# Down projection with its features on the partitions: wd stationary, activation moving, and the maxima over partitions by VectorE's 32x32 turns

## The reference

```python
gate = x @ W_gate.T + SCALE * (x @ A_gate.T) @ B_gate.T      # A, B by the entry's LoRA index, rank 16
up   = x @ W_up.T   + SCALE * (x @ A_up.T)   @ B_up.T        # 1376 wide
act  = silu(gate) * up
y    = act @ W_down.T + SCALE * (act @ A_down.T) @ B_down.T  # back to 512 features
amax = clip(max(abs(y), axis=-1), 1e-5)                      # one maximum per token, over 512 features
out  = (y / amax) @ weight_2bit.T * (amax * weight_scale) + bias
return x + out
```

## Time and profile before

| | us |
|---|---|
| median of 3 runs | 931.65 (930.52 to 932.57) |
| the profiled execution, its own time | 931.64 |
| its span in the profile | 929.6 |
| TensorE matmuls busy | 892.0 (96%), 3954 matmuls |
| TensorE weight loads busy | 720.6 (78%) |
| VectorE busy | 351.4 (38%) |
| ScalarE busy | 254.4 (27%) |
| GpSimd busy | 79.3 (9%) |

### The profile page before, as it was taken

One profiled execution on the slowest core, in us unless ns is written; L12 is line 12 of the kernel. 1 busy time (PEld: TensorE's weight loads), 2 busy tenths in 40 slices (PEclk: granted clock), 3 DMA queues, 4 the chain that ended last, 5 costly groups with the idle time before them and its releaser, 6 DMA issues.

```text
span 929.6 us, 13785 instructions
## 1 busy us (share of the span) xinstructions
PE 892.0 (96%) x3954; PEld 720.6 (78%) x3954; DVE 351.4 (38%) x762; ACT 254.4 (27%) x448; POOL 79.3 (9%) x110
## 2 busy tenths in 40 slices
PE   4799899999999999999999999999999999999994
PEld 3678688888888888888888888888888888888873
DVE  3543346332542226332363224432254223532233
ACT  2432234211431124211242113421142213421111
POOL 0010002200110001200102001020012000200100
PEclk9899999999999999999999999999999999999998
DMA  3443231120221112111121101101121111100011
GB/s 119 115 132 94 87 85 55 49 52 24 52 57 35 28 29 58 48 41 29 31 55 40 43 23 52 49 23 43 26 55 51 40 28 29 37 12 23 23 35 49
DMA packets 45445, 45.38 MB, mean 49 GB/s; under 512 B 13168, under 2 KB 31984, under 8 KB 45392
## 3 DMA queue, kind: packets, MB, share of 16 engines
q1 hardware_dynamic: 43312, 41.98, 16.7%
q10 hardware_dynamic: 2080, 2.88, 1.0%
HBM read 36.44 MB, written 8.39 MB: 48 GB/s over the span
## 4 chain that ended last, share of the span: by engine, by line
PE 91%; DVE 2%; SPq 2%; DMA 2%; ACT 1%; issue 1%; DVEq 0%; ACTq 0%
PE pp_up L1746 25%; PE pp_gate L1746 23%; PE pp_down L1823 23%; PE ps_misc L1850 5%; PE ps_td L1812 4%; PE ps_misc L1746 2%; PE pp_down L1833 2%; PE pp_up L1793 2%; PE pp_gate L1793 2%; PE ps_misc L1841 1%; DMA rows<-w_gu 1%; SPq L337 1%; DMA x_raw<-x_feat 0%; DMA b_raw<-places 0%; SPq L351 0%
## 5 line engine op out<-in xcount | busy, mean ns | idle before, releaser
L1823 PE MATMUL pp_down<-wd,actp_split 128*128 128x512 f32 x960 | 233.4, 392 | 0.0
L1746 PE MATMUL pp_up<-xw,wgu 128*128 128x512 f32 x948 | 229.3, 391 | 0.0
L1746 PE MATMUL pp_gate<-xw,wgu 128*128 128x512 f32 x864 | 213.6, 396 | 4.5 <-ACT actp_full L968 4.4
L1823 PEld LDWEIGHTS pp_down<-wd,actp_split 128*128 128x128 f32 x960 | 180.4, 188 | 45.0
L1746 PEld LDWEIGHTS pp_up<-xw,wgu 128*128 128x128 f32 x948 | 178.4, 188 | 38.4
L1746 PEld LDWEIGHTS pp_gate<-xw,wgu 128*128 128x128 f32 x864 | 161.2, 189 | 39.1 <-issue 5.7
L1412 DVE TENSOR_TENSOR actp_full<-pp_up,actp_full 128x512 f32<-128x512 f32 (+1 forms) x87 | 60.1, 691 | 329.7 <-PE pp_up L1793 313.4
L968 ACT ACTIVATE actp_full<-pp_gate 128x512 f32<-128x512 f32 (+1 forms) x80 | 47.7, 596 | 286.5 <-PE pp_gate L1793 274.9
L984 ACT ACTIVATE actp_split<-actp_full 128x512 fp32r<-128x512 f32 x80 | 50.6, 632 | 172.4 <-DVE actp_full L1412 172.4
L1421 DVE TENSOR_TENSOR actp_split<-actp_full,actp_split 128x512 fp32r<-128x512 f32 x80 | 55.2, 690 | 16.7 <-ACT actp_split L984 16.7
L1850 PE MATMUL ps_misc<-wq,dtp_split 128*128 128x512 f32 x232 | 57.5, 390 | 0.6 <-DVE dtp_split L1444 0.6
(11 more groups left out here) (112 smaller groups left out, 627.1 us busy)
## 6 DMA issues: line engine op xcount, KB each, us to landing
x_raw<-x_feat SPq DMA_DIRECT2D x122, 64.0 KB, 1.8
rows<-w_gu SPq DMA_DIRECT2D x8, 512.0 KB, 3.7
rows<-x_tok SPq DMA_DIRECT2D x64, 64.0 KB, 1.8
more_rows<-x_tok SPq DMA_DIRECT2D x64, 64.0 KB, 1.8
out<-rows SPq DMA_DIRECT2D x60, 64.0 KB, 1.6
out<-more_rows SPq DMA_DIRECT2D x60, 64.0 KB, 1.6
b_raw<-b_rows SPq DMA_DIRECT2D x32, 92.0 KB, 2.8
b_raw<-b_rows SPq DMA_DIRECT2D x32, 80.0 KB, 2.5
```

The lines of the kernel that those rows point to most:

```text
L1746: return nc.tensor.matmul(ps_out[0:m, a:b], w, xw[:, part, k, a:b], start=start, stop=stop)
L1823: last = nc.tensor.matmul(pp_down[:, s, :], actp_split[0:w, ap, f % 2, s * P:(s + 1) * P], wd[0:w, wp, f, :], start=(f == 1 and n == 0), s ...
```

## The change

`wide_down` and `down_first_and_lora` swap their operands: a 128x128 block of wd is stationary and the activation of all 512 tokens moves. A bank of pp_down (index h) then holds 128 output features on the partitions and 512 tokens along the row, the layout in which `ffn` takes its stationary operand. The count of matmuls and of their columns stays. The `transposes`, the identity's load and ScalarE's `normalise_rows` are gone.

The maximum per token now runs across partitions. VectorE takes it over the four banks (`feature_maxima`: a reduction of 2048 elements per partition to 512), turns 32x32 blocks, reduces 512 to 16, then joins the four groups of partitions (`token_maxima`), and turns the reciprocals back over the partitions (`spread_rinv`); four multiplications scale the banks (`normalise_chunk`). Its scratch is more_rows, so the residual rows of groups 2 and 3 are now loaded behind it (`residual_behind_scratch`, which waits for norm_ready; scratch_free tells VectorE that more_rows is stored). In the last tile the scratch is x_raw. `hi_norm` and `lo_norm` split from SBUF, at f = 2, 4, 6, 8; `ffn` stays at f = 3, 5, 7, 9. `store_wide` reads its entry numbers ahead of its wait.

```diff
+        hidden = rows[:, 0:KC, :]
...
+            entries = [wide_entry_at(eng, tile, (s * P + at) // SEQ) for at in rows_from]
             eng.wait_ge(out_ready, WIDE_SUBS * tile + s + 1)
-            for at in rows_from:
-                entry = wide_entry_at(eng, tile, (s * P + at) // SEQ)
+            for at, entry in zip(rows_from, entries):
...
+            def residual_behind_scratch(tile):
+                entries = [wide_entry_at(sp, tile, e) for e in range(2 * P // SEQ, WIDE_ENTRIES)]
+                sp.wait_ge(norm_ready, KC * tile + KC)
+                for n, entry in enumerate(entries):
+                    s, at = 2 + n * SEQ // P, n * SEQ % P
+                    sp.dma_start(res_rows(s)[at:at + SEQ, :], x_tok[bass.ds(entry, 1), :, :]
+                                 .rearrange("a t n -> (a t) n")).then_inc(res_in[s], 16)
...
-            def normalise_rows(tile, s, source):
-                act.wait_ge(rinv_ready, WIDE_SUBS * tile + s + 1)
-                nc.scalar.activation(norm_rows(s), source, ACT.Copy, scale=rinv[:, s:s + 1]).then_inc(norm_ready, 1)
...
-            def hi_transposed(tile, s, ps_block, dt):
-                act.wait_ge(transposed, WIDE_SUBS * tile + s + 1)
-                nc.scalar.activation(dt[:, 0, :, :], ps_block.rearrange("p (k t) -> p k t", k=KC),
-                                     ACT.Copy).then_inc(dt_hi, 1)
...
+            def drain(tile, h):
+                act.wait_ge(blocks_done, KC * tile + h + 1)
+                nc.scalar.activation(hidden[:, h, :], pp_down[:, h, :], ACT.Copy).then_inc(drained, 1)
...
+            def hi_norm(tile, s, dt):
+                last = isinstance(tile, int) and tile == WIDE_TILES - 1
+                act.wait_ge(norm_ready, KC * tile + (s + 1 if last else KC))
+                if s > 0 and not last:
+                    act.wait_ge(ffn_done, WIDE_SUBS * tile + s)
+                nc.scalar.activation(dt[:, 0, :, :], hidden[:, :, s * P:(s + 1) * P], ACT.Copy).then_inc(dt_hi, 1)
...
+            def feature_maxima(tile):
+                over_chunks, turned = scratch_columns(tile, 0), scratch_columns(tile, 1)
+                if not (isinstance(tile, int) and tile == WIDE_TILES - 1):
+                    dve.wait_ge(scratch_free, tile + 1)
+                dve.wait_ge(drained, KC * tile + KC)
+                maxima_step(tile, 1, nc.vector.tensor_reduce(over_chunks, hidden.rearrange("p h t -> p t h"), AX_X,
+                                                             ALU.max, apply_absolute_value=True))
+                maxima_step(tile, 2, nc.vector.transpose(turned, over_chunks))
+                maxima_step(tile, 3, nc.vector.tensor_reduce(group_max, turned.rearrange("p (c i) -> p c i", i=SEQ),
+                                                             AX_X, ALU.max))
...
+            def token_maxima(tile):
+                for g in range(KC):
+                    last = nc.vector.tensor_copy(by_group[:, g, :], group_max[g * SEQ:(g + 1) * SEQ, :])
+                maxima_step(tile, 4, last)
+                maxima_step(tile, 5, nc.vector.tensor_reduce(token_max, by_group.rearrange("p g c -> p c g"), AX_X,
+                                                             ALU.max))
+                maxima_step(tile, 6, nc.vector.tensor_scalar(token_max, token_max, EPS, None, ALU.max))
+                for g in range(KC):
+                    last = nc.vector.reciprocal(token_rinv[g * SEQ:(g + 1) * SEQ, :], token_max)
+                maxima_step(tile, 7, last)
...
+            def row_scales(tile):
+                for g in range(KC):
+                    nc.vector.tensor_scalar(ascale[g * SEQ:(g + 1) * SEQ, :], token_max[:, g:WIDE_ENTRIES:KC],
+                                            wscale[0:SEQ, :], None, ALU.mult).then_inc(ffn_scaled, 1)
+            def spread_rinv(tile):
+                over_rows, turned = scratch_columns(tile, 0), scratch_columns(tile, 1)
+                maxima_step(tile, 8, nc.vector.tensor_copy(turned.rearrange("p (c i) -> p c i", i=SEQ),
+                                                           token_rinv.unsqueeze(2).to_broadcast([P, WIDE_ENTRIES, SEQ])))
+                maxima_step(tile, 9, nc.vector.transpose(over_rows, turned))
+            def normalise_chunk(tile, h):
+                nc.vector.tensor_tensor(hidden[:, h, :], hidden[:, h, :], scratch_columns(tile, 0), ALU.mult
+                                        ).then_inc(norm_ready, 1)
+            def normalise_last(tile, s):
...
-                scales(tile - 1, 1, None)
                 lo_act(tile, 1)
                 ad(tile, 1)
+                feature_maxima(tile - 1)
...
-                        if f in (2, 3):
-                            scales(tile - 1, f, None)
                         lo_act(tile, f)
                         ad(tile, f)
+                    if f == 2:
+                        token_maxima(tile - 1)
+                        spread_rinv(tile - 1)
+                        for h in range(KC):
+                            normalise_chunk(tile - 1, h)
+                        row_scales(tile - 1)
...
                 w = WIDTHS[f]
-                for s in range(WIDE_SUBS):
+                for h in range(KC):
                     if f == 1 and not (isinstance(tile, int) and tile == 0):
-                        pe.wait_ge(drained, WIDE_SUBS * tile - WIDE_SUBS + s + 1)
+                        pe.wait_ge(drained, KC * tile - KC + h + 1)
                     for n, (ap, wp) in enumerate(PASSES):
-                        last = nc.tensor.matmul(pp_down[:, s, :], actp_split[0:w, ap, f % 2, s * P:(s + 1) * P],
-                                                wd[0:w, wp, f, :], start=(f == 1 and n == 0), stop=False)
+                        last = nc.tensor.matmul(pp_down[:, h, :], wd[0:w, wp, f, h * P:(h + 1) * P],
+                                                actp_split[0:w, ap, f % 2, :], start=(f == 1 and n == 0), stop=False)
                 last.then_inc(down_done, 1)
...
-            def transposes(tile, s, ps_block):
-                pe.wait_ge(norm_ready, WIDE_SUBS * tile + s + 1)
-                for k in range(KC):
-                    last = nc.tensor.transpose(ps_block[:, k * P:(k + 1) * P], norm_rows(s)[:, k * P:(k + 1) * P],
-                                               pair_identity)
-                last.then_inc(transposed, 1)
...
-                        transposes(tile - 1, s, ps_misc[:, :])
-                    if not first and f in (3, 5, 7, 9):
-                        ffn(tile - 1, f // 2 - 1, ps_misc[:, :], dtp_split)
+                        ffn(tile - 1, s, ps_misc[:, :], dtp_split)
...
+                    for s in (2, 3):
+                        sp.wait_ge(stored_rows[s], 16 * 4 * (tile - 1))
+                    sp.sem_inc(scratch_free, 1)
...
+                feature_maxima(tile)
+                token_maxima(tile)
+                spread_rinv(tile)
+                normalise_last(tile, 0)
                 for s in range(WIDE_SUBS):
-                    scales(tile, s, pp_down[:, s, :])
-                    if s > 0:
-                        lo_transposed(tile, s - 1, last_bank(s - 1), last_dt(s - 1))
-                lo_transposed(tile, WIDE_SUBS - 1, last_bank(WIDE_SUBS - 1), last_dt(WIDE_SUBS - 1))
+                    if s < WIDE_SUBS - 1:
+                        normalise_last(tile, s + 1)
+                    lo_norm(tile, s, last_dt(s))
+                row_scales(tile)
```

More of the change, by code:

```diff
@@ L76 @@
 WARM_UP = 24
+MAXIMA_STEPS = 9
 PLAN_COLUMNS_STEP = 8
@@ L186, in build, with scratch_columns @@
         td_lo_part = b_raw[STACK:P, 4 * H:4 * H + WIDE]
-        def norm_rows(s):
-            return rows[:, s, :]
+        hidden = rows[:, 0:KC, :]
+        def scratch_columns(tile, n):
+            if isinstance(tile, int) and tile == WIDE_TILES - 1:
+                return x_raw[:, n * KC:(n + 1) * KC, :].rearrange("p e n -> p (e n)")
+            return more_rows[:, n, :]
         def res_rows(s):
@@ L235, in build @@
         stored = sem("stored")
+        scratch_free = sem("scratch_free")
         wgu_hi = sem("wgu_hi")
@@ L631, in pair_program @@
                 sp.wait_ge(wq_ready, KC)
-                for s in range(WIDE_SUBS):
+                for s in range(2):
                     load_wide_residual(0, s)
+                sp.sem_inc(scratch_free, 1)
                 with sp.Fori(2, WIDE_TILES) as tile:
@@ L644, in pair_program @@
                     load_mask(tile - 1, mask_d, mask_d_in)
+                    residual_behind_scratch(tile - 2)
                     sp.wait_ge(bd_ready, tile)
@@ L1051, in next_tile @@
                 hi_b(tile, 2)
-                normalise_rows(tile - 1, 0, norm_rows(0))
                 hi_act(tile, 1)
@@ L1057, in next_tile @@
                         hi_b(tile, f + 1)
-                    if f <= WIDE_SUBS:
-                        normalise_rows(tile - 1, f - 1, norm_rows(f - 1))
                     if f < FC - 1:
@@ L1062, in next_tile @@
```

(35 more changed lines are left out.)

53 lines of the change are left out of this document (17 added, 36 removed).

## The result

| | before | after |
|---|---|---|
| median time, us | 930.52 (929.0 to 932.57, 5 runs) | 921.97 (921.35 to 924.98, 5 runs) |
| ratio to before | 1 | 0.9914 (0.9894 to 0.9934) |
| the profiled execution: time, span | 931.64, 929.6 | 924.79, 923.0 |

A forecast was written before the change was run, and what follows sets the result against it. TensorE, busy in 96% of the span, was taken to bound the kernel. Span 929.6 - 13.7 (turns) + 2.9 (last rows) = 918.8 us, plus 2.04 outside the span: 920.8 us, range 917 to 927 (its own 918.5 to 923.5).

The forecast's parts named there:

- The turns: Loop, tiles 1 to 7: removing four TensorE turns at 28 places saves 0.49 us each, 13.7 us.
- rival D: Loop: TensorE, earlier by 0.49, waits for something that came just in time; gain given back, 934.5 us; chance 0.02.
- The swapped matmuls: Down groups with wd stationary: same count and streamed columns, so 0 (between -1.8 and +3.5 us).
- Rival C: Swapped matmuls stream faster with a repeated stationary block, 915.5 us, chance 0.05; or slower, 924.3, chance 0.05.
- VectorE's chain in a tile: Loop: the new maxima work ends 2.6 us before TensorE's first ffn needs it, so costs nothing.
- Rival A: VectorE's passes somewhat slower than taken, outlasting the 2.6 us of slack in each tile: 926.6 us; chance 0.13.
- rival B: First reduction pays for every element 2 KB apart; gain gone at 5.9 us, 957 at four times the price; chance 0.05.
- SyncE and GpSimd: Loop: residual loads moved behind norm_ready, and the gathers and stores queued behind them, stay hidden: 0.
- The last rows: Kernel's end, all on the path: +2.9 us, from +1.9 to +6.
- To the first ffn: Last rows: drain, maxima, small instructions, spread, turn, multiplication and splits leave TensorE idle 9 us; ffn starts at 916.2.
- The clock: Last rows: after the idle time the 1.2 GHz level costs the ffn groups 1.8 to 2.8 us, taken as 2.3.
- The stores: Last rows: stores are a chain, 7.3 us from first finished rows at 920.8 to last issue at 928.1.

## Why the prediction was right, and where it was not

- **The turns**, 28 x 0.49 = 13.7: right. The loop lost 14.2, of which 13.9 are the turns (put back, they cost 13.9) and 0.3 the shorter wait for the last split ahead of the lora group, [1.17] in the earlier trace rows and [0.85] now. No wait of TensorE took the turns' time back: rival D is refuted.
- **The swapped matmuls**, 0: right, 233.2 against 233.4 us. Rival C is refuted in both directions.
- **VectorE's chain in a tile**, at no cost with 2.6 us of slack: the cost was right, the slack was mis-sized. There were 0.45. The reduction took 3.87, not 2.28, the copies 0.17 and the reciprocals 0.25 each, not little beside 0.16; the spread at 0.43 and four multiplications in 2.5 gave some back. Rival A's mechanism was there, 0.5 us short of costing anything; one more pass of 0.7 did (3.0 us in the loop). I had taken the price of reading along the row for a read with a step, and left the step to rivals with chances of 0.13 and 0.05. The Trainium skill, page SBUF — State Buffer, note on cachelines under the ports, has the rule by which it had to be more: an access that crosses to a new 16-byte line pays a penalty. The traces agree in the direction: 2.29 along the row, 3.62 to 3.87 with the step, a factor of 1.6 to 1.7, far from the 2.6 at which rival B had the gain gone. That it is the lines, and not something else about the step, no run here tells.
- **SyncE and GpSimd**, 0: right. In tile 6 SyncE started the eight residual loads at 705.95. GpSimd waits for transfers in the loop; no wait of TensorE, VectorE or ScalarE there names one.
- **The last rows**, +2.9 (1.9 to 6): this step failed; it was +7.9. By the five traces with these last rows, against the one trace of before, it was between +6.8 and +8.4. Its mechanism was right (TensorE idle, low clock, a chain of stores), its terms were too small. To the end of the last issue 4.3 us are missing. *To the first ffn* 14.4 and not 12.2: the reduction 1.3, the small instructions 0.8 (2.24 from 898.27 to 900.51, where I had 1.4). From there to the first finished rows another 0.3. *The clock* was sized rightly: the four groups and their gaps lasted 10.1 us (9.0 to 10.4 in the five traces), 7.6 with the array kept busy, so 2.6 against a forecast of 1.8 to 2.8, and it hardly counted at the end. *The stores* 9.2 from the first finished rows to the end of the last issue (8.5 to 10.2 in the five traces), not 7.3: reading the entry numbers ahead of a single wait still leaves them between the stores of two groups, and taking them out gave 1.05; the cause of the rest is open. Another 0.7 came behind the last issue, but that piece is anywhere from 4.1 to 5.4 us in the nine traces with the new maxima, so it is not shown to be the change's. My own upper bound of 6 came from a low clock alone; it did not add the strided reduction, which I had priced for the loop but not for the place where every microsecond of it counts.
- **The sum**: -13.7 + 2.9 = -10.8, pieces -14.2 + 7.9 = -6.3. The median of 921.97 stands within 1.2 us of the 920.8 because the runs that were compared lay lower, before (930.52, forecast from 931.65) and after; tile 0 alone moves by up to 4.5 us from trace to trace. That the total was hit so closely is in part luck. That the kernel would be faster, and by what, was not.

## What to carry to other kernels

Price a new pass at each place where it runs, not once: the step's 1.6 us were hidden seven times in the loop, and its 1.3 us in the tail were all on the path. When a chain is moved behind other work, write down the slack that remains and test it with a small dose; here a forecast of 2.6 was 0.45. Where several chains end together (a clock, a queue of stores, a list on one engine), taking one away can show little (nothing for the clock here, 1 us for the entry numbers), and taking all away (4.1 us) shows only what they were worth together.

## What the runs showed of the hardware

- VectorE's reduction of 2048 float32 with a step of 2 KB took 3.62 us beside an idle TensorE and 3.84 to 3.87 beside a busy one (busy in the tail: 3.84); along the row 2.29 in both.
- Behind a wait of TensorE of 2.02 to 2.04 us the granted clock fell in four tiles of seven, and not in three. What tells them apart stays open. Behind one of 0.13 us it stayed up.
- Eight ffn matmuls behind that wait of 0.13 us took 2.11 us, in a stream 1.98.
- VectorE turns 128x512 float32 in blocks of 32x32 in 0.71 us, where a multiplication of the same size takes 0.69; four turns of 128x128 on TensorE lengthen its stream by 0.49.
